# Layer-norm statistics of the last four tiles of x1: from ScalarE's squares to VectorE's batch statistics, one tile a step

## What is computed

```python
x = x + tanh(g_xattn[0]) * xattn(layernorm(x), ctx, ctx, Wq, Wk, Wv, Wd)
x = x + tanh(g_ffn[0]) * ffn(layernorm(x), w_gate, s_wgate, w_up, s_wup, w_down, s_wdown, inv_gate, inv_up, inv_inter)

def layernorm(x):                 # eps = 1e-5
    return (x - mean(x)) / sqrt(var(x) + eps)
def ffn(x, ...):                  # x rounded to bfloat16
    qg, sg = dynamic_quant(x, inv_gate)      # scale = max|row| / 127, values rounded
    qu, su = dynamic_quant(x, inv_up)
    inter = silu(gemm(qg, sg, w_gate)) * gemm(qu, su, w_up)
    inter = clip(inter, -10, 10).astype(bfloat16)
    return gemm(dynamic_quant(inter, inv_inter), w_down)
```

## Time and profile before

| | us |
|---|---|
| median of 3 runs | 1479.5 |
| lowest and highest of them | 1479.43, 1481.12 |
| the profiled execution | 1474.84 |
| its span, first to last instruction | 1472.9 |
| mean granted clock of TensorE | 0.997 of full speed |

### The profile page before, as it was taken

One profiled execution on the slowest core, in us unless ns is written; L12 is line 12 of the kernel. 1 busy time (PEld: TensorE's weight loads), 2 busy tenths in 40 slices (PEclk: granted clock), 3 DMA queues, 4 the chain that ended last, 5 costly groups with the idle time before them and its releaser, 6 DMA issues.

```text
span 1472.9 us, 19153 instructions
## 1 busy us (share of the span) xinstructions
PE 1424.6 (97%) x7235; PEld 1167.6 (79%) x7248; DVE 1002.9 (68%) x1565; ACT 564.4 (38%) x865; POOL 614.9 (42%) x429
## 2 busy tenths in 40 slices
PE   7999999999999999999999999999999999998887
PEld 7888888888888888887878888888888888874443
DVE  5866675757576766667475757666566667578997
ACT  4424241414142323234542423232232324148995
POOL 3455242434343343441343433434333424243884
PEclk9999999999999999999999999999999999999999
DMA  8834243433425243437265242333343424455565
GB/s 289 264 98 114 78 109 72 109 80 94 102 69 120 65 107 81 104 85 215 95 186 138 68 104 67 92 83 88 86 95 76 106 65 109 85 170 196 129 130 100
DMA packets 327131, 166.52 MB, mean 113 GB/s; under 512 B 275200, under 2 KB 290048, under 8 KB 326656
## 3 DMA queue, kind: packets, MB, share of 16 engines
q1 hardware_dynamic: 324448, 154.29, 39.4%
q0 software_dynamic: 2592, 11.01, 4.5%
HBM read 132.74 MB, written 35.65 MB: 114 GB/s over the span
## 4 chain that ended last, share of the span: by engine, by line
PE 78%; DVE 12%; DMA 3%; issue 2%; POOL 2%; ACT 2%; SPq 1%; POOLq 0%; ACTq 0%; DVEq 0%
PE psum L569 16%; PE psum L571 16%; PE psum L570 16%; PE psum L623 8%; PE psum L658 8%; PE psum L660 7%; PE psum L659 7%; DVE psum L1638 2%; DVE vw_lo L1368 1%; DVE res L1685 1%; DMA acc<-in_x 1%; DMA wv_raw<-in_wv_t 1%; SPq L368 1%; DVE xg L1648 1%; POOL rot L1253 1%
## 5 line engine op out<-in xcount | busy, mean ns | idle before, releaser
L569 PE MATMUL psum<-xt_hi,wq_hi 128*128 128x512 f32 x1024 | 400.9, 391 | 1.5 <-DVE xt_lo L1368 1.5
L571 PE MATMUL psum<-xt_hi,wq_lo 128*128 128x512 f32 x1024 | 398.6, 389 | 0.0
L570 PE MATMUL psum<-xt_lo,wq_hi 128*128 128x512 f32 x1024 | 398.5, 389 | 0.0
L1225 POOL TENSOR_TENSOR wq_lo<-wq_raw,wq_hi 128x512 fp32r<-128x512 f32 x128 | 170.0, 1340 | 484.3 <-ACT wq_hi L932 484.0
L1529 DVE TENSOR_TENSOR acc<-psum,acc 128x512 f32<-128x512 f32 x224 | 151.4, 681 | 140.0 <-PE psum L660 140.0
L1253 POOL TENSOR_TENSOR rot<-rot 128x1024 f32<-128x1024 f32 x64 | 153.6, 2400 | 207.8 <-DVE rot L1472 207.0
L978 ACT ACTIVATE vw_hi<-psum 64x512 fp32r<-64x512 f32 x256 | 151.7, 593 | 191.6 <-PE psum L571 187.9
L569 PEld LDWEIGHTS psum<-xt_hi,wq_hi 128*128 128x128 f32 x1024 | 192.3, 188 | 40.8 <-DVE xt_lo L1368 1.7
L571 PEld LDWEIGHTS psum<-xt_hi,wq_lo 128*128 128x128 f32 x1024 | 192.2, 188 | 40.1
L570 PEld LDWEIGHTS psum<-xt_lo,wq_hi 128*128 128x128 f32 x1024 | 192.4, 188 | 39.2
L1368 DVE TENSOR_TENSOR vw_lo<-psum,vw_hi 64x512 fp32r<-64x512 f32 x256 | 175.5, 687 | 53.9 <-ACT vw_hi L978 47.7
(11 more groups left out here) (153 smaller groups left out, 1910.0 us busy)
## 6 DMA issues: line engine op xcount, KB each, us to landing
wq_raw<-in_wq_t SPq DMA_DIRECT2D x128, 256.0 KB, 4.4
wd_raw<-in_wd_t SPq DMA_DIRECT2D x128, 256.0 KB, 3.7
p_scratch<-prob SPq DMA_DIRECT2D x60, 256.0 KB, 2.0
pt_raw<-p_scratch SPq DMA_DIRECT2D x240, 64.0 KB, 2.5
acc<-in_x SPq DMA_DIRECT2D x16, 512.0 KB, 5.3
out_x<-acc SPq DMA_DIRECT2D x16, 512.0 KB, 4.7
xa<-out_x SPq DMA_DIRECT2D x16, 512.0 KB, 3.6
out_x<-res POOLq DMA_DIRECT2D x15, 512.0 KB, 5.5
```

Of the source, the lines that this page charges most:

```text
L569: pe.matmul(dst, a_hi, b_hi, start=start, stop=False)
L570: pe.matmul(dst, a_hi, b_lo, start=False, stop=False)
L571: return pe.matmul(dst, a_lo, b_hi, start=False, stop=stop)
L1225: pool.tensor_tensor(dst, full, hi.bitcast(F32), ALU.subtract).then_inc(done, 1)
```

## The change

The second half's last four tiles (12 to 15) get their mean and variance from VectorE, by statistics and aggregate. Tile 12's statistics stand at the end of VectorE's last_outputs, behind the copy of the gate scales; those of tiles 13, 14 and 15 at the end of steps 1, 2 and 3, behind up_rows. The aggregates stand in step 4, behind the variances, which now cover tiles 8 to 11 alone. ScalarE's four calls of deviations for these tiles go, and so do the two calls of means for them. ScalarE's root waits for four more increments of stat_done. The sums of the half rows are still made.

```diff
--- before.py
+++ after.py
@@ -1140,15 +1140,12 @@
                     down_columns()
                     evacuate_gate(0)
                     evacuate_up(0)
-                    deviations(1, BT)
                     round_rows(1)
-                    deviations(1, BT + 1)
                     rows(2)
                     evacuate_gate(1)
                     silu(0)
                     evacuate_up(1)
                     rows(3)
-                    deviations(1, BT + 2)
                 if half == 0:
                     copy_rows(1, 1)
                     normalise(3)
@@ -1213,10 +1210,8 @@
                     rows(s + 2)
                 if there(s - 1):
                     silu(s - 1)
-                if s == 3:
-                    deviations(1, HTILES - 1)
                 if s == 4:
-                    root(TILES + 2, slice(HTILES, TILES))
+                    root(TILES + 2 + BT, slice(HTILES, TILES))
 
 
         @block.gpsimd
@@ -1744,8 +1739,6 @@
                 if half == 0:
                     lower_rows(1, 2)
                 add(gg - 1, 11)
-                if half == 1:
-                    means(slice(HTILES + BT, HTILES + BT + 2), HALVES * GROUPS * OPG - 4)
                 add(gg - 1, 12)
                 if half == 0:
                     lower_rows(1, 3)
@@ -1761,9 +1754,10 @@
                 if half == 0:
                     means(slice(0, HTILES), GROUPS * OPG)
                 else:
-                    means(slice(HTILES + BT + 2, TILES), HALVES * GROUPS * OPG)
                     gate_rows(0)
                     dve.tensor_copy(gate_scales, v_ig[:, 0:GCOLS]).then_inc(vg_done, 1)
+                    dve.wait_ge(o_done, HALVES * GROUPS * OPG)
+                    statistics(HTILES + BT, acc[:, BT, :])
 
             def row_statistics(t):
                 dve.wait_ge(x_in[t], 16)
@@ -1850,8 +1844,11 @@
                     if s > 1:
                         gate_rows(s - 1)
                     up_rows(s - 1)
+                if 1 <= s < 4:
+                    statistics(HTILES + BT + s, acc[:, BT + s, :])
                 if s == 4:
-                    variances(slice(HTILES, TILES), TILES)
+                    variances(slice(HTILES, HTILES + BT), HTILES + BT)
+                    aggregate(slice(HTILES + BT, TILES), TILES + BT)
                 if s == 5:
                     second_norm(5, 1)
             last_rows(TILES - 1)
```

## The result

| | before | changed kernel |
|---|---|---|
| median of 11 runs each | 1479.51 | 1482.29 |
| lowest and highest | 1478.42, 1483.32 | 1479.44, 1486.1 |
| profiled execution: span | 1472.9 | 1480.0 |
| mean granted clock of TensorE in it | 0.997 | 0.993 |

The ratio lies within 0.2% of no change, and the median in the range; the forecast was 1.3 us slower, which is near the lower end of the interval.

The account below looks back on a forecast made before the run. VectorE was taken to set the pace in the tail's body, with waits in earlier steps. Terms -0.69 + 1.22 - 0.41 + 0.0 + 1.22 + 0.0 = 1.3 us, added to 1479.5, gave 1480.8; range 1478.4 to 1483.5.

Parts of the forecast that it names:

- Tiles 12 and 13 and the first two waits: VectorE to step 2: their statistics, 1.22 us each, nearly cancel against waits for yb(2) and xi(0); xi(0)'s reduction 0.12 later.
- the 1344.56: Predicted time at which VectorE is through with gate_rows(0) and the copy of the gate scales, 1344.65 before.
- the 0.69 of the sum: Gain at xg(2), predicted to start at 1345.78 instead of 1346.47 because yb of tile 2 comes earlier.
- Tile 14 hidden: Before up_rows(2): its 1.22 us fit in 1.73 us of waits, 0.51 to spare; up_rows(2) moves only 0.12.
- Tile 15 uncovered: Behind up_rows(2), step 4 has no VectorE wait, so its 1.22 us of statistics count in full.
- aggregates hidden: End of step 4: variances and four aggregates add 0.36 us, hidden by the 0.91 wait at up_rows(4).
- rival C: The clock doesn't fall, up(2) ends 1.3 us earlier and the sum is only +0.8: 1480.3; chance 0.10.
- The table load of Sqrt: ScalarE's 1.28 us load isn't behind the semaphore and covers the aggregates; otherwise 0.35 us would be added.
- Carried to the end: From the end of step 5 the loop is full on VectorE, 7.25 us per step, and carries the 1.3 us through.
- A: VectorE is saturated and no wait is filled: 4.9 us slower, 1484.4; chance 0.08.
- B: TensorE's low clock lasts over gate(2) and up(2), before up_rows(2): 2.7 us more, 4.0 in all, 1483.5; chance 0.08.
- D: ScalarE's chain paces all early steps and hides all statistics, leaving yb's 1.13 us gain: 1478.4; chance 0.10.

Follow-up runs that it names:

- e2: The changed kernel, unchanged, profiled once more in an execution with mean clock 0.997: 1481.72 us beside 1480.53 for the kernel before, ratio 1.000.
- e5: The kernel before with 25 extra matmuls on unread data where TensorE idles: 1475.05 us beside 1482.03, ratio 0.9958.
- e6: The changed kernel with 25 extra matmuls on unread data where TensorE idles, run again on another chip: 1475.72 us beside 1482.03, ratio 0.996.
- e1: The kernel before, unchanged, profiled once more: 1482.04 us beside 1480.53 for the same kernel, ratio 1.001.
- e8: The changed kernel with the 25 extra matmuls, without statistics and aggregates of tiles 12 to 15 on either engine: 1471.43 us beside 1482.03, ratio 0.9935.
- e11: The kernel before with only tile 14 on VectorE's statistics, tile 13's square behind rows(3), second_norm ahead of up_rows(4), no extra matmuls: 1475.21 us, ratio 0.9976.
- e3: The changed kernel with 25 extra matmuls on unread data where TensorE idles: 1474.3 us beside 1480.53 for the kernel before, ratio 0.9959.
- e4: The changed kernel with second_norm's six small instructions moved ahead of up_rows(4): 1477.81 us beside 1480.53 for the kernel before, ratio 0.9986.
- e9: The kernel before with second_norm's six small instructions moved ahead of up_rows(4): 1476.62 us beside 1480.59, ratio 0.9984.

## Why the prediction was right, point by point

**Tiles 12 and 13 and the first two waits.** The prediction let gate_rows(0) come 0.09 earlier, because the pair of means held it. That was misread: it starts 0.43 us behind the last read of the accumulator before (1342.46) and 0.45 in e2 (1342.50), 0.12 behind gate(0)'s end in both, with a wait of 0.36 for TensorE in place of the means. From gate_rows(0), the predicted times say xg(2) 0.60 earlier and the reduction of xi(0) 0.21 later. In e2: 0.72 earlier and 0.05 earlier. They more than cancel; a tile's statistics take 1.19 to 1.20 us from start to start, not 1.22, and the 1344.56 was an end, which the next instruction overlaps. That the 0.69 of the sum came out as 0.72 is luck: the two misreadings are of like size and opposite sign.

**Tile 14 hidden.** up_rows(2) at +20.21 in e2, against +20.25 before: held. The wait left was 0.64, of 0.51 predicted. (down(0) took 3.17 us there, the low clock having begun earlier, before 1354.)

**Tile 15 uncovered, aggregates hidden.** In e2 up_rows(4) at +36.93 against +35.78: 1.15 us, with a wait of 0.62 left (predicted 0.5 to 0.6). Step 6 at +38.78 against +37.64. The forecast's 1.3 is 1.15 at the measured sizes and, with the clock at its upper level throughout, 0.90 (e5, e6), where rival C had said 0.8: then up_rows(2) is no longer held by TensorE, and up_rows(3) of the kernel before has a wait of 0.50 that takes in part of tile 15. The table load of Sqrt ran as assumed: in e2 it began at 1372.35, while the aggregates ran until 1372.73, and Sqrt followed right behind it at 1373.64.

**Carried to the end.** From step 6 to the last instruction of VectorE the two profiles with a mean clock of 0.997, before and e2, take the same but for the last product: down(15) kept VectorE waiting 3.24 us in the profile before and 2.39 in e2, a matter of the clock. That is why their spans differ by 0.4 and not by 1.1. The product and the wait for it in the kernel before and in e2:

```profile
1465.55 3.27 PE L789 MATMUL psum<-wo,qi 128*128 128x512 bf16 x8 [0.69 <-ACT qi L1094]
...
1467.58 0.76 DVE L1828 SCALAR_TENSOR_TENSOR res<-psum,v_sd 128x512 f32<-128x512 f32 x1 [3.24 <-PE psum L789]
```

```profile
1466.74 1.90 PE L789 MATMUL psum<-wo,qi 128*128 128x512 bf16 x8 [0.69 <-ACT qi L1094]
...
1467.91 0.76 DVE L1822 SCALAR_TENSOR_TENSOR res<-psum,v_sd 128x512 f32<-128x512 f32 x1 [2.39 <-PE psum L789]
```

**The median.** 2.8 us in the first comparison, 1.2 in the second, in which the kernel before, put beside itself, read 1.5 us slower. The forecast of 1.3 fits both, but the second interval takes in no change at all: what bears the mechanism out is the count from wait to wait, not the medians. The excess of the first comparison is not settled. With the low clock in step 5 step 6 began at +43.15 in e1 and at +44.88 in the changed kernel, 1.7 later, but these are two executions with low stretches of different length. The prediction worked its 1.3 out on a profile of the rarer kind, with a mean clock of 0.997; that the other kind, 9 of 10 executions, gives a difference of like size (1.4 between the medians) was not foreseen in it and is in part luck.

**The rivals.** A is refuted by e8 and by the waits that went. B named the right mechanism in the wrong place and for the wrong kernel: the fall that costs most is in step 5, behind the idle time in which the copy of qi(2) waits for Sqrt and its table load, it was there before the change, and I had taken a profile at 0.997 as typical when 9 of 10 executions are below. I could have seen it in the 4.7 us between the profiled execution and the median, which I only added on. D is refuted by step 6, which came later (1.14 us in e2, 0.90 in e6) and not 1.1 earlier: tile 15 found no wait. What no rival had is the collision of second_norm with GpSimd, 2.6 us in both profiles in which the fall makes it.

## What to carry to other kernels

An engine's idle time can be filled wherever what ends the wait does not itself start from the added work; go from wait to wait and ask what chain releases each, and count only the piece that has no wait behind it. Before two profiles are compared, look at the granted clock of both: a profiled execution that is faster than the median of its own kernel is not the typical one, and its missing microseconds may be larger than the change. Where TensorE idles between short products, matmuls on constant data in the gaps are worth a trial: here they gave 6 to 7 us by the medians, the change of schedule nothing, and the better one of e11 5.4.

## What the runs showed of the hardware that was not expected

Twenty-five matmuls of 128x512 that nobody reads, about 6 us of TensorE's time by 0.24 each, took 6.2 us off the kernel (e3): down and gate behind the gaps ran at the upper clock level, and second_norm no longer met GpSimd. A VectorE instruction of 128x8 elements with two inputs in SBUF took up to 1.23 us beside GpSimd, and 0.17 when GpSimd stood still. The two met only in the profiles in which the clock had fallen in step 5 and second_norm stood behind up_rows(4). In these two the clock fell a third time, near 1392 in the changed kernel and near 1394 in e1; in e4, e9 and e11, which also fell in step 5 but have second_norm moved, that third low stretch did not come. It agrees with this that the 4 us of second_norm left TensorE idle for the next fall, but no run tests it alone.
